# Layer norms of a tower: all eight chunks in one group, with four rows in each of four blocks of 32 partitions

## The chip, the cores and the metric

The kernel runs on one core of a Trainium2 chip. The metric is the time of one execution on the device, in microseconds (us). The engines are named as the profile names them: PE is TensorE (matmuls), PEld its weight load, DVE is VectorE, ACT is ScalarE, POOL is GpSimd, SP is SyncE, which issues the DMAs of this kernel.

## What is computed

The reference is a tower of eight residual stages after a convolution with its normalization, on a tensor h of 4 batches, 746 positions and 128 channels. Ahead of each of the eight stages stands a plain layer norm over the 128 channels. Three of the steps hold a further layer norm with a gain and an offset for each channel: one at the end of the first mixture of experts, and one at the start and one at the end of the last. Cut to what the change touches:

```python
def layer_norm(x, g, b):
    m = x.mean(-1, keepdims=True)
    v = ((x - m) ** 2).mean(-1, keepdims=True)
    return (x - m) / jnp.sqrt(v + EPS) * g + b

h = _L0_tok_ref(x, ...)
h = h + _L0_attn_ref(_layernorm(h, axis=-1), ...)
h = h + _L0_ffn_ref(_layernorm(h, axis=-1), ...)
...
h = h + _L3_ffn_ref(_layernorm(h, axis=-1), ...)
```

## The kernel before

The activations lie with the channels on the 128 partitions: `hT` is 128 x 2984 (4 batches of 746), `zT` holds the normalized copy. A layer norm is a block of its own: `Alloc.clear` ends each block with a barrier over all engines (line 74), so nothing of the stage before or behind it runs beside it. There are eleven such blocks: eight plain ones (names `ln1` to `ln8` in the code, shown together as `ln_...` by the profile), `ln_ffn` and `ln_out` with gain, offset and an addition to `hT` (`add=True`), and `ln_in` with gain and offset, written to `zT`.

Within a block the 2984 columns are eight chunks of 373 (`HALF`), each of them half a batch. For a chunk, PE multiplies by the matrix `center`, which gives the deviations from the mean in a bank `d` of PSUM (line 233); ACT squares them to `sq` (line 274) and copies them to `dev` in SBUF (line 278); PE sums the squares over the channels with a weight of five columns, `avg_rows`, of which one is 1/128, so that chunk c of a group lands in row c of the tile `var` (line 240). When all chunks of a group are in, ACT takes the root of the whole tile (line 283) and DVE the reciprocal (line 302). PE then spreads row c over 128 partitions with a weight of 3 or 5 rows, `spread_rows` (line 252), into one of three banks `r_ps`, and DVE multiplies `dev` by it (line 308). With a gain and an offset DVE applies them next (line 312) and, with `add`, adds the result to `hT` (line 315).

The eight chunks are in two groups, `LN_GROUPS = ((0, 3), (3, 8))`. The order on each engine is written out by hand: the deviations of three chunks, the variances of group 0, further deviations, then the variances of group 1. The second group's chain runs beside the first one's. Everything is float32, and a float32 matmul stands in the profile as two records of MATMUL and two of LDWEIGHTS.

`load_constants` (line 99) is the first block of the program: SP loads five constants, DVE clears `zT`, and the next block's loads start behind its barrier.

## Time and profile before

| | |
|---|---|
| time, median of 3 runs | 3778.83 us (3778.07 to 3781.88) |
| time of the profiled execution | 3788.9 us |
| its span | 3786.8 us |
| PE busy | 3283.6 us, 87% of the span |
| DVE busy | 2044.3 us, 54% |
| ACT busy | 1478.5 us, 39% |
| mean granted TensorE clock | 0.894 of 2.4 GHz |

The span is the stretch in which the engines work; the time of the same execution is 2.1 us more. Busy shares are means over stages with different limits. PE's busy time counts a matmul from its start to its modelled end, so matmuls in a pipeline overlap, and their starts tell more of their pace than their durations do. A granted clock of 1.00 is 2.4 GHz, 0.50 is 1.2 GHz.

### The profile page before, as it was taken

How to read it: one execution, taken by the hardware profiler on the slowest of the kernel's cores; microseconds unless marked ns; L12 is line 12 of the kernel's file. 1: busy time of each engine (PE TensorE's matmuls, PEld its weight loads, DVE VectorE, ACT ScalarE, POOL GpSimd, SP SyncE). 2: the span in 40 equal slices, each digit the busy share in tenths (PEclk: the TensorE clock that was granted, in tenths of full speed). 3: DMA queues.
4: the chain of work that ended last, by engine and by line, in shares of the span. 5: the costliest groups of instructions: out<-in, count | busy, mean ns of one | idle time of the engine just before them, and what ended most of it. 6: DMA issues, size and time to landing. Idle time of an engine off the chain costs nothing. (4 is left out here: it accounts for less than half of the span.)

```text
span 3786.8 us, 48812 instructions
## 1 busy us (share of the span) xinstructions
PE 3283.6 (87%) x15986; PEld 2080.6 (55%) x15986; DVE 2044.3 (54%) x4128; ACT 1478.5 (39%) x2951; POOL 25.2 (1%) x56
## 2 busy tenths in 40 slices
PE   6399999995799989977598869999859999977997
PEld 3244444443577768834254446666536666645775
DVE  3355665662499981054314347776646777743223
ACT  2145555542244431122241215555415555533443
POOL 0000000000000000000000000000000000000000
PEclk8599999996799999978696669999969999977998
DMA  2344444430111110000010031222023333201110
GB/s 83 113 132 136 137 133 140 134 122 22 48 45 67 44 35 18 0 2 0 11 34 0 0 128 61 75 107 112 10 79 81 70 71 75 51 2 69 45 67 19
DMA packets 138473, 243.98 MB, mean 64 GB/s; under 512 B 44389, under 2 KB 106215, under 8 KB 132548
## 3 DMA queue, kind: packets, MB, share of 16 engines
q1 hardware_dynamic: 130982, 232.85, 19.3%
q10 hardware_dynamic: 7360, 9.44, 0.8%
q8 instruction: 75, 1.23, 0.1%
q14 instruction: 56, 0.46, 0.0%
HBM read 147.39 MB, written 57.67 MB: 54 GB/s over the span
## 5 line engine op out<-in xcount | busy, mean ns | idle before, releaser
L1176 PE MATMUL moe_o_ps<-moe_hid,moe_w 128*128 128x373 f32 x1152 | 387.6, 479 | 14.2 <-DVE moe_hid L1244 14.2
L398 PE MATMUL moe_h_ps<-stage_z_part,moe_wh 128*128 128x374 f32 x1152 | 340.0, 376 | 5.2 <-ACT stage_y L1191 1.7
L2111 ACT ACTIVATE lstm_gate<-lstm_g_ps,lstm_bias 128x373 f32<-128x373 f32 x368 | 209.8, 573 | 250.2 <-PE lstm_g_ps L2072 236.5
L894 DVE TENSOR_REDUCE rel_nmax<-rel_s_ps 128x1 f32<-128x746 f32 x192 | 179.1, 933 | 197.6 <-PE rel_s_ps L751 153.1
L1176 PEld LDWEIGHTS moe_o_ps<-moe_hid,moe_w 128*128 128x128 f32 x1152 | 216.1, 190 | 126.6 <-issue 18.5
L2710 DVE TENSOR_REDUCE caus_nmx<-caus_a_ps 128x4 f32<-128x512 f32 (+5 forms) x352 | 215.8, 641 | 107.5 <-PE caus_a_ps L2526 104.8
L858 ACT ACTIVATE rel_probs<-rel_s_ps,rel_nmax 128x746 f32<-128x746 f32 x192 | 169.7, 884 | 258.0 <-DVE rel_nmax L894 153.2
L2072 PE MATMUL lstm_g_ps<-lstm_state,lstm_w 128*128 128x373 f32 x640 | 254.6, 480 | 6.7 <-DVE lstm_state L2194 4.1
L1202 ACT ACTIVATE moe_ex<-moe_h_ps,moe_w 128x373 f32<-128x373 f32 x320 | 173.1, 574 | 221.2 <-PE moe_h_ps L398 219.7
L2661 ACT ACTIVATE caus_probsT<-caus_s_ps 128x512 f32<-128x512 f32 (+4 forms) x352 | 189.6, 558 | 150.8 <-PE caus_s_ps L2545 147.1
L398 PEld LDWEIGHTS moe_h_ps<-stage_z_part,moe_wh 128*128 128x128 f32 x1152 | 209.8, 192 | 55.3 <-DVE moe_hid L1244 12.8
L2066 PE MATMUL lstm_g_ps<-lstm_xm,lstm_w 128*128 128x373 f32 x512 | 202.3, 477 | 0.0
L1229 DVE TENSOR_TENSOR moe_part<-moe_o_ps,moe_gate 128x373 f32<-128x373 f32 x144 | 78.1, 542 | 229.0 <-PE moe_o_ps L1176 229.0
L1244 DVE SCALAR_TENSOR_TENSOR moe_hid<-moe_h_ps,moe_w,moe_ex 128x373 f32<-128x373 f32 x320 | 194.0, 606 | 11.3
L398 PE MATMUL moe_h_ps<-stage_z_part,moe_wl 128*128 128x374 f32 x576 | 194.8, 338 | 0.0
L1204 ACT ACTIVATE moe_hid<-moe_h_ps,moe_w 128x373 f32<-128x373 f32 x256 | 135.4, 573 | 144.6 <-PE moe_h_ps L398 144.6
L2526 PE MATMUL caus_a_ps<-caus_ks,caus_qs 96*128 96x128 f32 (+6 forms) x768 | 180.2, 326 | 10.5 <-DVE caus_nmx L2710 10.5
L2545 PE MATMUL caus_s_ps<-caus_qs,caus_ks 98*128 98x128 f32 (+6 forms) x768 | 186.3, 333 | 0.5 <-ACT caus_probsT L2661 0.4
L762 PE MATMUL rel_t_ps<-tower_ident,rel_probs 128*128 128x128 f32 x1152 | 167.4, 284 | 4.5 <-DVE rel_probsT L657 4.5
L2072 PEld LDWEIGHTS lstm_g_ps<-lstm_state,lstm_w 128*128 128x128 f32 x640 | 122.1, 191 | 87.1 <-DVE lstm_state L2194 4.7
L398 PE MATMUL shared_h_ps<-stage_z_part,shared_w1h 128*128 x576 | 147.6, 338 | 13.2 <-DVE shared_w1l L390 13.0
L789 PE MATMUL rel_o_ps<-rel_probsT,rel_v_pad 128*32 128x373 f32 x768 | 150.8, 501 | 0.2 <-issue 0.2
(385 smaller groups left out, 5677.0 us busy)
## 6 DMA issues: line engine op xcount, KB each, us to landing
moe_gate<-gates SPq DMA_DIRECT2D x18, 1536.0 KB, 7.0
lstm_row<-gates SPq DMA_DIRECT2D x16, 1536.0 KB, 13.4
caus_qs<-caus_xh SPq DMA_DIRECT2D x128, 93.2 KB, 2.1
caus_ks<-caus_xh SPq DMA_DIRECT2D x128, 93.2 KB, 2.1
moe_w<-in_moe_w SPq DMA_DIRECT2D x18, 514.0 KB, 3.6
lstm_row<-gates SPq DMA_DIRECT2D x8, 1152.0 KB, 7.4
rel_shear<-rel_probs SPq DMA_DIRECT2D x32, 256.0 KB, 3.0
rel_bias<-rel_r_sb SPq DMA_DIRECT2D x32, 255.0 KB, 2.0
```

Source lines behind the costliest of these rows:

```text
L398: mm = nc.tensor.matmul(out, w[i], x[j], start=(start and n == 0), stop=(stop and n == len(terms) - 1))
L894: nc.vector.tensor_reduce(nmax[now.slot][:, t:t + 1], s_ps[t % 2][:, 0:L], AX.X, ALU.max, negate=True).then_inc(max_ready, 1)
L1176: mm = nc.tensor.matmul(o_ps[i % 2][:, 0:HALF], w[s][:, HID + j * P:HID + (j + 1) * P], hid[i % 2][:, j, :], start=(j == 0), stop=(j == HJ ...
L1202: nc.scalar.activation(ex[j][:], h_ps[j][:, 0:HALF], ACT.Exp, bias=b1).then_inc(ex_done, 1)
L1244: nc.vector.scalar_tensor_tensor(out=hid[i % 2][:, j, :], in0=h_ps[j][:, 0:HALF], scalar=w[s][:, 2 * HID + j:2 * HID + j + 1], in1=ex[j][: ...
L2066: mm = nc.tensor.matmul(bank, w[e % 2][:, g * P:(g + 1) * P], z, start=True, stop=(s == 0))
L2072: mm = nc.tensor.matmul(bank, w[e % 2][:, 4 * P + g * P:4 * P + (g + 1) * P], state[e % 2][k or 0][i][:], start=False, stop=True)
L2111: nc.scalar.activation(gate[x % 3][g][:], g_ps[n % RING][:, 0:HALF], ACT.Tanh if g == 2 else ACT.Sigmoid, bias=b[:, e, g:g + 1]).then_inc( ...
L2526: mm = nc.tensor.matmul(out[:, at, :], qs[s][0:K_S, hh, t * P:q1], ks[s][0:K_S, hh, k0:k1], start=not diag, stop=not diag or hh == HPG - 1)
L2545: mm = nc.tensor.matmul(out[:, at, :], ks[s][0:K_T, hh, j * P:k1], qs[s][0:K_T, hh, q0:q1], start=not diag, stop=not diag or hh == HPG - 1)
L2661: nc.scalar.activation(probsT[j][0:rows, heads[0]:heads[-1] + 1, q0 - j * P:q1 - j * P], heads_of(s_ps[at % 3][0:rows, :], heads, q1 - q0) ...
L2710: nc.vector.tensor_reduce(nmx[0:rows, slot, heads[0]:heads[-1] + 1, t:t + 1], heads_of(bank[0:rows, :], heads, k1 - k0), AX.X, ALU.max, ne ...
```

## The change

A block has one group of all eight chunks. A chunk's 373 columns are cut into two halves of 187 (`SUB`), the second starting at column 186 (`SUB_AT`). The tile `var` is now 128 partitions by 187 columns: chunk c = 4g + j has its two halves in rows 32j + 2g and 32j + 2g + 1, so each block of 32 partitions holds four rows that are used. The weight of the variance, `avg_sel`, has 32 columns, and its four matmuls of a row (j = 0 to 3) write to the four blocks of 32 partitions. There is one root and one reciprocal, of 128 x 187. To spread a chunk, PE takes 32 rows of `spread_sel` and of `rstd`, in two matmuls of 187 columns, into one of four banks `r_ps`; the banks `d` are three instead of four. The copies from `d` to `dev` are moved from ACT to DVE, and each waits for its chunk's square. With a gain, `spread_sel` is replaced by a tile of the block that holds the gain in place of the ones (128 x 512, loaded in the block), and the offset is added by DVE together with `hT` in one instruction (line 307 of the changed kernel), or by ACT for `ln_in` (line 286). `load_constants` clears the two selection tiles on DVE first, SP waits for that, and then fills them with five small loads in place of two.

```diff
-LN_GROUPS = ((0, 3), (3, 8))
+SUB_AT = HALF // 2
+SUB = HALF - SUB_AT
...
-            for name in ("center", "avg_rows", "spread_rows"):
-                sp.dma_start(K[name][:], io[name]).then_inc(loaded, 16)
-            sp.wait_ge(loaded, 80)
+            sp.dma_start(K["center"][:], io["center"]).then_inc(loaded, 16)
+            sp.wait_ge(cleared, 2)
+            sp.dma_start(K["avg_sel"][:, :, 0:4], io["avg_rows"][:, 0:4, 0:4]).then_inc(loaded, 16)
+            for j in range(4):
+                sp.dma_start(K["spread_sel"][32 * j:32 * j + 4, :, :], io["spread_rows"][0:4, 0:4, :]).then_inc(loaded, 16)
+            sp.wait_ge(loaded, 128)
...
+            nc.vector.memset(K["avg_sel"][:], 0.0).then_inc(cleared, 1)
+            nc.vector.memset(K["spread_sel"][:], 0.0).then_inc(cleared, 1)
             nc.vector.memset(K["zT"][:], 0.0).then_inc(filled, 1)
...
-def layer_norm(nc, K, name, src="hT", affine=None, affine_d=None, add=False):
+def layer_norm(nc, K, name, src="hT", affine_d=None, add=False):
...
-    D, R = 4, 3
+    D, G = 3, 4
+    N = len(CHUNKS)
+    rows_of = 2 * (N // G)
...
-        sd = [a.sb(f"sd{g}", [GROUP_MAX, HALF]) for g in range(2)]
-        rstd = [a.sb(f"rstd{g}", [GROUP_MAX, HALF]) for g in range(2)]
+        sd = a.sb("sd", [P, SUB])
+        rstd = a.sb("rstd", [P, SUB])
+        spread_sel = K["spread_sel"] if affine_d is None else a.sb("spread_scale", [P, rows_of, P])
+        beta = None if affine_d is None else a.sb("beta", [P, 1])
         d = [a.ps(f"d{i}", [P, BANK]) for i in range(D)]
-        var = a.ps("var", [GROUP_MAX, BANK])
-        r_ps = [a.ps(f"r_ps{i}", [P, BANK]) for i in range(R)]
+        var = a.ps("var", [P, BANK])
+        r_ps = [a.ps(f"r_ps{i}", [P, BANK]) for i in range(G)]
...
-            if affine is not None:
-                sp.dma_start(affine[:], affine_d).then_inc(cols_in, 16)
+            if affine_d is not None:
+                sp.dma_start(beta[:], affine_d[1]).then_inc(beta_in, 16)
+                sp.dma_start(spread_sel[:], affine_d[0]).then_inc(scale_in, 16)
...
-            def variance(g, c):
-                first, end = LN_GROUPS[g]
-                pe.wait_ge(sq_ready, c + 1)
-                if g > 0 and c == first:
-                    pe.wait_ge(sd_ready, g)
-                mm = nc.tensor.matmul(var[:, 0:HALF], K["avg_rows"][:, c - first, :], sq[c][:], start=(c == first),
-                                      stop=(c == end - 1))
-                if c == end - 1:
+            def variance(g):
+                pe.wait_ge(sq_ready, (g + 1) * G)
+                for m in range(2):
+                    row = 2 * g + m
+                    for j in range(G):
+                        mm = nc.tensor.matmul(var[32 * j:32 * j + 32, 0:SUB], K["avg_sel"][:, row, :],
+                                              sq[g * G + j][:, m * SUB_AT:m * SUB_AT + SUB], start=(row == 0),
+                                              stop=(row == rows_of - 1))
+                if g == N // G - 1:
                     mm.then_inc(var_ready, 1)
-            def spread_row(g, c):
-                first, end = LN_GROUPS[g]
-                if c == first:
-                    pe.wait_ge(rstd_ready, g + 1)
-                if c >= R:
-                    pe.wait_ge(scaled, c - R + 1)
-                n = end - first
-                nc.tensor.matmul(r_ps[c % R][:, 0:HALF], K["spread_rows"][0:n, c - first, :], rstd[g][0:n, :],
-                                 start=True, stop=True).then_inc(spread, 1)
-            for c in range(LN_GROUPS[0][1]):
+            def spread_row(c):
+                g, j = divmod(c, G)
+                if g > 0:
+                    pe.wait_ge(scaled, c - G + 1)
+                for m in range(2):
+                    nc.tensor.matmul(r_ps[j][:, m * SUB_AT:m * SUB_AT + SUB], spread_sel[32 * j:32 * j + 32, 2 * g + m, :],
+                                     rstd[32 * j:32 * j + 32, :], start=True, stop=True).then_inc(spread, 1)
+            for c in range(0, 5):
                 deviations(c)
-            for c in range(LN_GROUPS[0][1]):
-                variance(0, c)
-            for c in range(D - 1, N - 1):
+            variance(0)
+            for c in range(5, N):
                 deviations(c)
-            variance(1, D - 1)
-            deviations(N - 1)
-            for c in range(D, N):
-                variance(1, c)
-            for g in range(2):
-                for c in range(*LN_GROUPS[g]):
-                    spread_row(g, c)
+            variance(1)
+            if affine_d is not None:
+                pe.wait_ge(scale_in, 16)
+            pe.wait_ge(rstd_ready, 1)
+            for c in range(N):
+                spread_row(c)
...
-            def squares(c0, c1):
-                for c in range(c0, c1):
-                    act.wait_ge(d_ready, c + 1)
-                    nc.scalar.activation(sq[c][:], d[c % D][:, 0:HALF], ACT.Square).then_inc(sq_ready, 1)
-            def copies(c0, c1):
-                for c in range(c0, c1):
-                    nc.scalar.copy(dev[c][:], d[c % D][:, 0:HALF]).then_inc(copied, 1)
-            def roots(g):
-                act.wait_ge(var_ready, g + 1)
-                n = LN_GROUPS[g][1] - LN_GROUPS[g][0]
-                nc.scalar.activation(sd[g][0:n, :], var[0:n, 0:HALF], ACT.Sqrt, bias=K["eps5"][0:n, 0:1]).then_inc(sd_ready, 1)
-            squares(0, LN_GROUPS[0][1])
-            copies(0, LN_GROUPS[0][1])
-            roots(0)
-            squares(LN_GROUPS[0][1], D)
-            copies(LN_GROUPS[0][1], D)
-            squares(D, N)
-            roots(1)
-            copies(D, N)
+            def squares(c):
+                act.wait_ge(d_ready, c + 1)
+                nc.scalar.activation(sq[c][:], d[c % D][:, 0:HALF], ACT.Square).then_inc(sq_ready, 1)
+            for c in range(N):
+                squares(c)
+            act.wait_ge(var_ready, 1)
+            nc.scalar.activation(sd[:], var[:, 0:SUB], ACT.Sqrt, bias=K["eps5"][:, 0:1]).then_inc(sd_ready, 1)
+            if affine_d is not None and not add:
+                act.wait_ge(beta_in, 16)
+                for c, (b, half) in enumerate(CHUNKS):
+                    act.wait_ge(scaled, c + 1)
+                    nc.scalar.activation(z_chunk(zT, b, half), xn[c % 2][:], ACT.Identity, bias=beta[:, 0:1]).then_inc(moved, 1)
...
-            if affine is not None:
-                dve.wait_ge(cols_in, 16)
-            link = Chain(dve, chain)
-            for g, (first, end) in enumerate(LN_GROUPS):
-                n = end - first
-                dve.wait_ge(sd_ready, g + 1)
-                nc.vector.reciprocal(rstd[g][0:n, :], sd[g][0:n, :]).then_inc(rstd_ready, 1)
-            for c, (b, half) in enumerate(CHUNKS):
-                dve.wait_ge(spread, c + 1)
-                x = xn[c % 2][:]
-                out = z_chunk(zT, b, half) if affine is None else x
+            def copies(c):
+                dve.wait_ge(sq_ready, c + 1)
+                nc.vector.tensor_copy(dev[c][:], d[c % D][:, 0:HALF]).then_inc(copied, 1)
+            def multiply(c):
+                b, half = CHUNKS[c]
+                out = z_chunk(zT, b, half) if affine_d is None else xn[c % 2][:]
                 dve.wait_ge(copied, c + 1)
-                nc.vector.tensor_tensor(out, dev[c][:], r_ps[c % R][:, 0:HALF], ALU.mult).then_inc(scaled, 1)
-                if affine is not None:
-                    dve.wait_ge(scaled, c + 1)
-                    out = x if add else z_chunk(zT, b, half)
-                    link.link(nc.vector.tensor_scalar(out, x, affine[:, 0:1], affine[:, 1:2], ALU.mult, ALU.add))
-                    if add:
-                        h = h_chunk(hT, b, half)
-                        link.link(nc.vector.tensor_tensor(h, h, x, ALU.add))
+                dve.wait_ge(spread, 2 * (c + 1))
+                if affine_d is not None and c > 1:
+                    dve.wait_ge(moved, c - 1)
+                nc.vector.tensor_tensor(out, dev[c][:], r_ps[c % G][:, 0:HALF], ALU.mult).then_inc(scaled, 1)
+            def add_to_h(c):
+                b, half = CHUNKS[c]
+                h = h_chunk(hT, b, half)
+                dve.wait_ge(scaled, c + 1)
+                nc.vector.scalar_tensor_tensor(h, xn[c % 2][:], beta[:, 0:1], h, ALU.add, ALU.add).then_inc(moved, 1)
+            def finish_chunk(c):
+                multiply(c)
+                if add and c > 0:
+                    add_to_h(c - 1)
+            for c in range(N):
+                copies(c)
+            if add:
+                dve.wait_ge(beta_in, 16)
+            dve.wait_ge(sd_ready, 1)
+            nc.vector.reciprocal(rstd[:], sd[:]).then_inc(rstd_ready, 1)
+            for c in range(N):
+                finish_chunk(c)
+            if add:
+                add_to_h(N - 1)
...
-            "avg_rows": a.sb("avg_rows", [P, GROUP_MAX, GROUP_MAX]),
-            "spread_rows": a.sb("spread_rows", [GROUP_MAX, GROUP_MAX, P]),
+            "avg_sel": a.sb("avg_sel", [P, 4, 32]),
+            "spread_sel": a.sb("spread_sel", [P, 4, P]),
...
+def spread_scale(g):
+    out = np.zeros((P, 4, P), np.float32)
+    for m in range(4):
+        out[m::32, m, :] = g
+    return out
```

Left out are the hunks that only pass the gain and the offset from the host in two arrays.

On PE, the first plain layer norm, between the token convolution and the attention. Before:

```order
L233 MATMUL ln_d<-tower_hT,tower_center 128x373 x3
L240 MATMUL ln_var<-ln_sq,tower_avg_rows 5x373 x3
L233 MATMUL ln_d<-tower_hT,tower_center 128x373 x4
L240 MATMUL ln_var<-ln_sq,tower_avg_rows 5x373
L233 MATMUL ln_d<-tower_hT,tower_center 128x373
L240 MATMUL ln_var<-ln_sq,tower_avg_rows 5x373 x4
L252 MATMUL ln_r_ps<-ln_rstd,tower_spread_rows 128x373 x8
```

With the change:

```order
L239 MATMUL ln_d<-tower_hT,tower_center 128x373 x5
L246 MATMUL ln_var<-ln_sq,tower_avg_sel 32x187 x8
L239 MATMUL ln_d<-tower_hT,tower_center 128x373 x3
L246 MATMUL ln_var<-ln_sq,tower_avg_sel 32x187 x8
L257 MATMUL ln_r_ps<-ln_rstd,tower_spread_sel 128x187 x16
```

Five deviations come ahead of the first variances, the eight variance matmuls of 373 columns are sixteen of 187, in two runs of eight, and the eight spreads are sixteen of half the width.

On DVE, the last layer norm, at the end of the program. Before (rows 3 to 5 then come for each chunk):

```order
L302 RECIPROCAL ln_out_rstd<-ln_out_sd 3x373
L302 RECIPROCAL ln_out_rstd<-ln_out_sd 5x373
L308 TENSOR_TENSOR ln_out_xn<-ln_out_dev,ln_out_r_ps 128x373
L312 TENSOR_SCALAR ln_out_xn<-ln_out_xn,stage_ln_cols 128x373
L315 TENSOR_TENSOR tower_hT<-tower_hT,ln_out_xn 128x373
```

With the change (the last two rows then alternate to the end):

```order
L292 COPY ln_out_dev<-ln_out_d 128x373 x8
L319 RECIPROCAL ln_out_rstd<-ln_out_sd 128x187
L301 TENSOR_TENSOR ln_out_xn<-ln_out_dev,ln_out_r_ps 128x373 x2
L307 SCALAR_TENSOR_TENSOR tower_hT<-ln_out_xn,ln_out_beta,tower_hT 128x373
L301 TENSOR_TENSOR ln_out_xn<-ln_out_dev,ln_out_r_ps 128x373
```

The eight copies come to DVE, one reciprocal goes, and a chunk has two instructions behind the reciprocal instead of three; the addition of a chunk stands behind the multiply of the next.

## Rows read from the trace of the kernel before

**Rows 1.** The page: the span, and each engine's busy time.

```profile
span 3786.8 us, 48812 instructions
...
PE 3283.6 (87%) x15986; PEld 2080.6 (55%) x15986; DVE 2044.3 (54%) x4128; ACT 1478.5 (39%) x2951; POOL 25.2 (1%) x56
```

**Rows 2.** Line 308, eight plain norms: what it waited for (us, times).

```profile
  PE ln_r_ps L252: 19.5, 30
```

**Rows 3.** Timeline, first norm A: start, duration (us), engine, work, idle before, releaser.

```profile
46.99 4.07 PE L233 MATMUL ln_d<-tower_hT,tower_center 128*128 128x373 f32 x6 [5.89 <-PEq L74]
...
57.43 2.67 PE L240 MATMUL ln_var<-ln_sq,tower_avg_rows 128*5 128x373 f32 x8
...
60.14 0.56 ACT L283 ACTIVATE ln_sd<-ln_var,tower_eps 5x373 f32<-5x373 f32 x1 [2.12 <-PE ln_var L240]
...
63.14 2.70 DVE L308 TENSOR_TENSOR tower_zT<-ln_dev,ln_r_ps 128x373 f32<-128x373 f32 x5
...
69.02 0.54 DVE L308 TENSOR_TENSOR tower_zT<-ln_dev,ln_r_ps 128x373 f32<-128x373 f32 x1 [0.70 <-PE ln_r_ps L252]
```

**Rows 4.** Timeline, the plain norm B at 1796.5 us.

```profile
1796.57 2.12 PE L233 MATMUL ln_d<-tower_hT,tower_center 128*128 128x373 f32 x6 [1.52 <-PEq L74]
1797.47 1.74 ACT L274 ACTIVATE ln_sq<-ln_d 128x373 f32<-128x373 f32 x3 [11.79 <-PE ln_d L233]
...
1808.16 2.48 DVE L302 RECIPROCAL ln_rstd<-ln_sd 5x373 f32<-5x373 f32 x1 [3.45 <-ACT ln_sd L283]
```

**Rows 5.** Timeline, `ln_out`: table load and root, a chunk on DVE, the end.

```profile
3756.76 1.28 ACT L283 ACT_TABLE_LOAD   x1
...
3764.58 2.48 DVE L302 RECIPROCAL ln_out_rstd<-ln_out_sd 5x373 f32<-5x373 f32 x1 [3.37 <-ACT ln_out_sd L283]
...
3766.99 0.47 DVE L308 TENSOR_TENSOR ln_out_xn<-ln_out_dev,ln_out_r_ps 128x373 f32<-128x373 f32 x1
...
3768.59 0.55 DVE L308 TENSOR_TENSOR ln_out_xn<-ln_out_dev,ln_out_r_ps 128x373 f32<-128x373 f32 x1
...
3779.72 0.55 DVE L315 TENSOR_TENSOR tower_hT<-tower_hT,ln_out_xn 128x373 f32<-128x373 f32 x1
```

**Rows 6.** Timeline, `ln_in`: its second reciprocal and its last instruction.

```profile
3389.50 2.48 DVE L302 RECIPROCAL ln_in_rstd<-ln_in_sd 5x373 f32<-5x373 f32 x1 [4.30 <-ACT ln_in_sd L283]
...
3400.05 0.48 DVE L312 TENSOR_SCALAR tower_zT<-ln_in_xn,stage_ln_cols 128x373 f32<-128x373 f32 x1
```

**Rows 7.** Stretches of norms A and B: us, busy times, then PEclk (granted clock), DMA.

```profile
46.96:51.40 4.44, 4.41 (x7) 1.94 (x8) 0.00 (x0) 1.27 (x3) 0.00 (x0) 0.50 0.00 0
51.60:65.10 13.50, 11.91 (x37) 4.61 (x36) 6.70 (x6) 6.32 (x15) 0.00 (x0) 1.00 0.00 0
65.20:69.57 4.37, 3.79 (x7) 1.51 (x5) 2.18 (x4) 0.00 (x0) 0.00 (x0) 0.50 0.00 0
1796.54:1812.70 16.16, 14.54 (x43) 6.01 (x44) 6.80 (x6) 8.68 (x19) 0.00 (x0) 1.00 0.00 1
```

**Rows 8.** Lines of other stages with like work: ns minimum/median/maximum, starts, shapes.

```profile
L2742 DVE RECIPROCAL caus_r<-caus_su x128: 679/727/741, 2871.7 to 3344.3; 128x93 f32<-128x93 f32 x96, 128x94 f32<-128x94 f32 x32
...
L906 DVE COPY rel_o_sb<-rel_o_ps x16: 539/540/541, 238.4 to 861.6; 64x373 f32<-64x373 f32 x16
...
L1890 DVE SCALAR_TENSOR_TENSOR tower_hT<-picked_eo,stage_weight_cols,tower_hT x16: 606/607/610, 1887.4 to 1964.9; 128x373 f32<-128x373 f32 x16
...
L2651 ACT COPY caus_su<-caus_a_ps x32: 354/471/586, 2865.2 to 3339.7; 128x512 f32<-128x512 f32 x16, 128x234 f32<-128x234 f32 x16
```

**Rows 9.** Timeline, PE in the causal attention, at clock 1.00.

```profile
2923.42 1.40 PE L2561 MATMUL caus_o_ps<-caus_probsT,caus_v_tok 128*32 128x128 f32 x32
```

**Rows 10.** Timeline, the program's start.

```profile
1.47 2.62 DVE L117 MEMSET tower_zT<- 128x3080 f32 x1 [1.47 <-PEq L2831]
...
2.61 0.38 SPq L112 DMA_DIRECT2D tower_spread_rows<-in_spread_rows  x1
...
4.99 0.36 SPq L143 DMA_DIRECT2D tok_w<-in_tok_w  x1
```

More of the change, by code:

```diff
@@ L103, in load_constants @@
         loaded = a.sem("loaded")
+        cleared = a.sem("cleared")
         filled = a.sem("filled")
@@ L1427, in stage2 @@
         shared_conv(nc, io, K, y, z_parts)
-        layer_norm(nc, K, "ln_ffn0", src=y, affine=cols, affine_d=io["ln_ffn0"], add=True)
+        layer_norm(nc, K, "ln_ffn0", src=y, affine_d=(io["ln_ffn0_g"], io["ln_ffn0_b"]), add=True)
 STAGES[2] = stage2
@@ L1536, in _ @@
                 dve.wait_ge(done, B)
-        layer_norm(nc, K, "ln_out3", src=y, affine=cols, affine_d=io["ln_out3"], add=True)
+        layer_norm(nc, K, "ln_out3", src=y, affine_d=(io["ln_out3_g"], io["ln_out3_b"]), add=True)
 STAGES[8] = stage8
@@ L1547, in stage8_layout @@
         "moe3_b2": f["L3_ffn_b2"],
-        "ln_in3": np.stack([f["L3_ffn_ln_g"], f["L3_ffn_ln_b"]], 1),
-        "ln_out3": np.stack([f["L3_ffn_out_g"], f["L3_ffn_out_b"]], 1),
+        "ln_in3_g": spread_scale(f["L3_ffn_ln_g"]),
+        "ln_in3_b": f["L3_ffn_ln_b"][:, None],
+        "ln_out3_g": spread_scale(f["L3_ffn_out_g"]),
+        "ln_out3_b": f["L3_ffn_out_b"][:, None],
     }
```

14 lines of the change are left out of this document (6 added, 8 removed).

## The prediction

> **What bounds the kernel now.** I read the page first. PE is busy for 3283.6 of 3786.8 us and DVE for 2044.3 [rows 1], but the change touches only the eleven layer norms, which stand between barriers, so shares over the whole span say nothing here. The question is how long each norm's own chain is: what it saves there is saved in full, since nothing runs beside it.
>
> So the timelines of the norms come next. Norm A, the first, starts at 46.99 and ends at 69.02 + 0.54 = 69.56: 22.6 us. Its chain has three parts [rows 3]. The front runs from the first matmul to the second root, which starts at 60.14, 13.15 us in. On it PE is nearly always at work: the last eight records of the variance start at 57.43, and the root follows 2.71 us later. Then root and second reciprocal: 0.56 and 2.48 us. Then the tail, 69.56 − (60.14 + 0.59 + 2.48) = 6.35 us, in which five multiplies take 2.70 us without a pause and the last waits 0.70 us for PE.
>
> Norm B starts with PE at 2.4 GHz, and its first square starts 0.90 us after the first matmul; its second reciprocal starts 11.6 us in [rows 4], where A's starts 13.7 us in. The stretches say why: A's first 4.4 us have a granted clock of 0.50, B's first 16 us have 1.00. In A the clock is back at 0.50 for the last 4.4 us [rows 7], and there the multiplies wait for PE: the eight plain norms wait 19.5 us in all, 30 times [rows 2].
>
> In `ln_out` the tail is 3780.27 − 3767.06 = 13.2 us, because DVE has three instructions for a chunk, one chunk each (3768.59 − 3766.99) = 1.60 us at the start [rows 5]. In `ln_in`, with two instructions, it is 3400.53 − 3391.98 = 8.55 us [rows 6].
>
> **The front.** A float32 matmul of 373 columns is two records. The eight variance records of A take 2.67 us and B's first six 2.12 [rows 3, 4]: both fit 0.31 us for a record and some 0.2 us of modelled end behind the last, so 0.62 us for a matmul. At a clock of 0.50 it is twice that, 1.24 us: A's first six records take 4.07 us.
>
> The variance goes from 8 x 0.62 = 5.0 us to sixteen matmuls of 187 columns, which in a row would take the same 5.0 us. But they lie in four blocks of 32 columns of the array. The causal attention has such work: 32 records of 128 x 128, with 32 columns of weight, in 1.40 us [rows 9]; in a row they would take 32 x 128 / 373 x 0.31 = 3.4 us and more. So four blocks do run at the same time there. By that row a run of eight matmuls (16 records of 187 columns) takes 16/32 x 1.22 (without the last end) x 187/128 = 0.9 us at most; four at a time exactly would be 0.63 us. I take 0.65 us, for the order of the loops is the same, j inside. That is 1.3 us instead of 5.0 for both runs, but PE now waits for squares, which it did not before.
>
> I walk through B with the new order. Deviations 0 to 2 end at 1.9 us. The fourth needs bank 0 free: square 0 ends at 0.9 + 0.5 = 1.4, and the copy, now on DVE and behind the square, costs 0.54 us by a like copy from PSUM [rows 8], so 2.0; it ends at 2.7, the fifth at 3.35. Square 3 ends at 3.5, the first variances run from 3.6 to 4.3, deviations 5 to 7 from 4.4 to 6.3, square 7 from 6.6 to 7.1, the second variances from 7.2 to 7.85. The root can start at 8.1. Before it stood at 11.0 (0.59 us ahead of the reciprocal, as in A): 2.9 us less. In A, where the clock rises near 4.5 us, the fifth deviation ends at 5.4, deviation 7 at 8.3, square 7 at 9.1, and the root starts at 10.1 instead of 13.15: 3.0 us less. One thing is late next: in seven norms ACT loads a table of 1.28 us for the root [rows 5]. Before, it lay beside the first group's work; now it starts at the end of square 7, and the root at 7.1 + 1.3 = 8.4. So I take −3.0 for four norms and −2.7 for seven: **−30.9 us**. If the copies on DVE cost twice as much they would still end ahead of PE's other work in A, and cost 0.5 us in B.
>
> **Root and reciprocal.** On ACT, 512 columns take 586 ns and 234 take 354 [rows 8], 0.83 ns a column, so 186 fewer columns are 0.15 us less: **−1.7 us** over eleven. The reciprocal is 2.48 us for 373 columns whether 3 or 5 partitions, and 0.72 for 93 with 128 partitions [rows 4, 8]; on the line between, 187 columns cost 1.31 us. One instead of two, and the first was beside other work: −1.17 each, **−12.8 us**.
>
> **The tail.** All eight spreads now stand behind the reciprocal, where three of them were ahead of it. The first multiply waits for 0.62 us of matmul and its way through, 1.0 us in all, by B's first square [rows 4]. That is a cost that was not there. Behind it the multiplies follow one another if PE keeps up: 2.70 / 5 = 0.54 us each [rows 3], 4.3 us for eight. PE needs 0.63 us for a chunk at full clock if its matmuls run one after another, and less if chunks overlap. The chunks lie in four blocks of rows, and no row of this trace shows blocks of rows beside one another; only blocks of columns are shown. Bounds: 0.16 us a chunk with four at a time, 0.63 at 2.4 GHz in a row, 1.25 at 1.2 GHz in a row. I take overlap, since rows 9 are the nearest. Then the plain tail is 5.35 us. Before it was 6.35 in A; over eight norms the multiplies waited 19.5 / 8 = 2.4 us each [rows 2], and 4.3 + 2.4 less the overlap at the first is 6.6 us. **−1.25 x 8 = −10.0 us**.
>
> The Trainium skill, page "TensorE: Matmul & The Clock Gate", section "Part 3: Packing small matmuls — row/col tiling", says the same of rows: four tiles of 32 rows ran 3.07 times as fast as one after another. By the Trainium skill's figure a chunk would cost 0.63 / 3.07 = 0.2 us, an estimate; one after another it is 0.63. No row here shows blocks of rows, and the sum is made without that figure.
>
> With `add` a chunk is 0.57 us of multiply and 0.61 + 0.02 of the fused addition [rows 8], 1.2 x 8 + 1.0 = 10.7 us against 13.2: **−5.0 us** for two. In `ln_in` the offset moves to ACT beside the next multiply: 1.0 + 8 x 0.57 + 0.65 = 6.3 against 8.55: **−2.2 us**. The gains' load is issued as the block starts and needed eight microseconds later, so it costs nothing; without that cover it would be some 3 us three times.
>
> **The constants.** Before, the last of five loads is issued at 2.61 and the next block's first at 4.99; the clearing of `zT` ends at 4.09 [rows 10], so both paths were level. Now 640 columns are cleared first, by 2.62 us for 3080 columns some 0.6 us; SP goes on at 2.15, issues five loads 0.47 us apart, the last at 4.1 instead of 2.61: **+1.5 us**.
>
> **The sum**: −30.9 − 1.7 − 12.8 − 10.0 − 5.0 − 2.2 + 1.5 = −61.1 us. The profiled execution (3788.9 us, its span and 2.1 us around it) would become 3727.8. The median of the runs shown is 10.1 us lower, and the same difference gives 3778.8 − 61.1 = **3718 us**. Chance of this case 0.70. By its own bounds it lies between 3706 (a chunk in B-like norms always at full clock, the front 0.5 us shorter each) and 3736.
>
> **Rivals.** *The spreads run one after another, and the clock falls in the tail* (0.13). For it: no row shows blocks of rows at the same time, and PE idles for some 2.1 us before the spreads, the root and the reciprocal. Against: in A the clock held from 4.6 to 18.1 us [rows 7], longer than the new norm lasts. With every spread at 1.25 us the plain tail is 1.7 + 7 x 1.25 + 0.55 = 11.0 us, +4.4 against before, so eight plain norms give back 45 us, and the others 5: 3768 us. With half of the tails so, 3743.
>
> *The column blocks do not overlap* (0.05): each of the two runs takes 2.5 us instead of 0.65, +3.7 us a norm, 3759 us. Rows 9 speak against it. This is the case in which the change does not do what it says, since the packed layout would buy only the shorter reciprocal.
>
> *No change that can be told* (0.04): the first rival in full and a fifth of the second, 3776 us.
>
> *Slower* (0.04): one mechanism, PE stays at 1.2 GHz in the whole norm because it now works in short bursts, and spreads in a row. Eight deviations take 9.9 us, the root starts at 14.0 instead of 13.15 (or 11.0, in a norm like B), the plain tail is 11.0: about +1.3 at the front, −1.3, +4.4, so +4.4 a plain norm, +4 over the three others, +1.5: 3819 us. It decides from about 1.3 us for a spread chunk on: below that the front's 3 us and the reciprocal pay for the tail. B's sixteen microseconds at 1.00 with pauses in them speak against it.
>
> *More than forecast* (0.04), below 3706: the clock is high in more norms, since they are shorter.
>
> **The numbers.** Range 3704 to 3746, which holds the forecast's own bounds and half of the first rival. A difference under 0.2%, 7.6 us, is about what a measurement of this kernel can't tell from none: 3771.3 to 3786.4. Faster 0.92, same 0.04, slower 0.04.
>
> **What would show it.** In the profile after: roots in norms like A near 10.1 to 10.4 us after the first matmul; a reciprocal near 1.3 us; variance records in runs of eight matmuls of 0.65 us and its pipeline end; multiplies 0.54 to 0.57 us apart with no wait for PE but the first; token weights asked for near 6.5 us instead of 4.99. The forecast is wrong if multiplies wait for the spreads, if the copies on DVE hold up the deviations, or if the granted clock is 0.50 over whole norms.

## The result and the profile after

The changed kernel takes 3728.45 us (median of four runs, 3726.81 to 3733.92), the kernel before 3780.36 us beside it: a ratio of 0.9863, with a 95% interval of 0.9846 to 0.9880, so 51.9 us less. The forecast was 3718 us, with a range of 3704 to 3746.

The page of the changed kernel, to be read beside [rows 1]:

```profile
span 3732.1 us, 49417 instructions
...
PE 3216.6 (86%) x16290; PEld 2084.7 (56%) x16338; DVE 2039.7 (55%) x4183; ACT 1446.7 (39%) x2860; POOL 25.2 (1%) x56
```

The profiled execution took 3733.92 us, 55.0 less than that of before, and its span is 54.7 us shorter. DVE's busy time hardly moves: in each norm eight copies come to it, while two long reciprocals become one short one. The eleven norms, each from its first matmul to its last instruction, add up to 199.1 us instead of 258.4. So the norms give 59.3 us, and 4.6 us are given back outside them.

The timeline of the norm that answers to B [rows 4]. At the end of a row stands the idle time of the engine before it, and what ended it:

```profile
1779.80 3.54 PE L239 MATMUL ln_d<-tower_hT,tower_center 128*128 128x373 f32 x10 [1.48 <-PEq L75]
...
1783.29 0.84 PE L246 MATMUL ln_var<-ln_sq,tower_avg_sel 128*32 128x187 f32 x16
1784.06 2.15 PE L239 MATMUL ln_d<-tower_hT,tower_center 128*128 128x373 f32 x6
...
1786.75 1.28 ACT L281 ACT_TABLE_LOAD   x1
...
1786.79 0.84 PE L246 MATMUL ln_var<-ln_sq,tower_avg_sel 128*32 128x187 f32 x16 [0.57 <-ACT ln_sq L276]
1788.05 0.42 ACT L281 ACTIVATE ln_sd<-ln_var,tower_eps 128x187 f32<-128x187 f32 x1
1788.49 1.33 DVE L319 RECIPROCAL ln_rstd<-ln_sd 128x187 f32<-128x187 f32 x1 [1.18 <-ACT ln_sd L281]
...
1789.88 1.65 PE L257 MATMUL ln_r_ps<-ln_rstd,tower_spread_sel 32*128 32x187 f32 x16 [2.25 <-DVE ln_rstd L319]
1791.60 1.90 DVE L301 TENSOR_TENSOR tower_zT<-ln_dev,ln_r_ps 128x373 f32<-128x373 f32 x4 [1.78 <-PE ln_r_ps L257]
...
1793.92 1.90 DVE L301 TENSOR_TENSOR tower_zT<-ln_dev,ln_r_ps 128x373 f32<-128x373 f32 x4 [0.42 <-PE ln_r_ps L257]
```

The root starts 1788.05 − 1779.80 = 8.25 us after the first matmul (forecast 8.4) and the reciprocal takes 1.33 us (1.31). Sixteen variance records take 0.84 us with their end. Then the surprise: the first multiply waits 1.78 us behind the reciprocal, not 1.0, and the fifth waits 0.42. The first four multiplies start (1.90 − 0.54) / 3 = 0.45 us apart.

Stretches of 1 us at the first spreads, in six of the eleven norms (columns as in [rows 7]):

```profile
62.00:63.00 1.00, 1.00 (x12) 1.00 (x16) 0.00 (x0) 0.00 (x0) 0.00 (x0) 0.50 0.08 16
909.50:910.50 1.00, 0.86 (x16) 0.57 (x16) 0.07 (x1) 0.00 (x0) 0.00 (x0) 1.00 0.00 0
...
1789.90:1790.90 1.00, 1.00 (x12) 1.00 (x16) 0.00 (x0) 0.00 (x0) 0.00 (x0) 0.50 0.00 0
1953.30:1954.30 1.00, 1.00 (x12) 1.00 (x16) 0.00 (x0) 0.00 (x0) 0.00 (x0) 0.50 0.00 0
...
2719.10:2720.10 1.00, 0.86 (x16) 0.57 (x16) 0.07 (x1) 0.00 (x0) 0.00 (x0) 1.00 0.00 0
...
3715.50:3716.50 1.00, 0.94 (x16) 0.66 (x16) 0.02 (x1) 0.00 (x0) 0.00 (x0) 1.00 0.00 0
```

The number right behind the five busy times, the granted clock, is 0.50 in three of these rows. Of all eleven norms, seven are so, and four have 1.00. Where it is 1.00, the first multiply waits 1.06 to 1.13 us and a plain tail takes 5.28 us; where it is 0.50, 1.78 to 1.84 and 6.00. What line 301 (the multiply) waited for over the plain norms (us, times), beside 19.5 and 30 in [rows 2]:

```profile
  PE ln_r_ps L257: 15.8, 17
```

In `ln_out` the clock was 1.00 at the spreads, and DVE alone sets the pace, 1.20 us a chunk instead of 1.60 [rows 5]:

```profile
3718.12 0.54 DVE L301 TENSOR_TENSOR ln_out_xn<-ln_out_dev,ln_out_r_ps 128x373 f32<-128x373 f32 x1
3718.59 0.60 DVE L307 SCALAR_TENSOR_TENSOR tower_hT<-ln_out_xn,ln_out_beta,tower_hT 128x373 f32<-128x373 f32 x1
3719.32 0.55 DVE L301 TENSOR_TENSOR ln_out_xn<-ln_out_dev,ln_out_r_ps 128x373 f32<-128x373 f32 x1
```

The start of the program, beside [rows 10]; the load of `tok_w` is issued 1.1 us later than before:

```profile
2.62 1.43 SPq L117 DMA_DIRECT2D tower_spread_sel<-in_spread_rows  x4
...
6.10 0.36 SPq L150 DMA_DIRECT2D tok_w<-in_tok_w  x1
```

The terms in us, summed over the eleven norms of the two profiled executions (the measured sum is that of the unrounded terms). The front runs from the first matmul to the root, the tail from the end of the reciprocal to the last instruction:

| term | forecast | measured |
|---|---|---|
| front, to the (second) root | −30.9 | −32.1 |
| root | −1.7 | −1.5 |
| reciprocal | −12.8 | −12.7 |
| tail, eight plain norms | −10.0 | −6.3 |
| tail, `ln_ffn` and `ln_out` | −5.0 | −5.1 |
| tail, `ln_in` | −2.2 | −1.7 |
| outside the norms | +1.5 | +4.6 |
| sum | −61.1 | −54.7 |

### The profile page after: what moved, and what is told of

The parts are those of the page before. It is cut to its first block and busy times, and to the rows that moved or that the text cites. A ratio compares the mean times of both kernels' runs of the same rounds, so it can differ in the third digit from the quotient of the medians.

```text
span 3732.1 us, 49417 instructions
## 1 busy us (share of the span) xinstructions
PE 3216.6 (86%) x16290; PEld 2084.7 (56%) x16338; DVE 2039.7 (55%) x4183; ACT 1446.7 (39%) x2860; POOL 25.2 (1%) x56
## 5 line engine op out<-in xcount | busy, mean ns | idle before, releaser
L406 PEld LDWEIGHTS moe_h_ps<-stage_z_part,moe_wh 128*128 128x128 f32 x1152 | 210.0, 192 | 54.9 <-DVE moe_hid L1252 12.8
L406 PE MATMUL shared_h_ps<-stage_z_part,shared_w1h 128*128 x576 | 148.2, 339 | 12.4 <-DMA shared_b<-in_sh_b 12.4
```

Source lines behind the costliest of these rows:

```text
L406: mm = nc.tensor.matmul(out, w[i], x[j], start=(start and n == 0), stop=(stop and n == len(terms) - 1))
```

## The experiments

The theory after the first comparison is that both kinds of blocks overlap, and that the plain tail was mis-sized because PE idles before the spreads and then runs them at 1.2 GHz. A rival for the late first multiply is a cost of the row blocks themselves. Each edit is made to the changed kernel. A ratio is to the kernel before on the same chip, whose median there was 3786.3 us (`col_serial`, `row_serial`, `fill_pe`, `whole_consts`), 3792.0 (`change_again`, `best`, `copies_act`, `one_group_rows`) or 3790.5 (`fill_one`, `offset_apart`) and not 3780.4, so ratios are compared, and medians only within such a set; sums over the norms are against the changed kernel's first profile.

**col_serial**: the variance's weight is 128 columns wide, so its matmuls can't lie beside one another.

```diff
-    mm = nc.tensor.matmul(var[32 * j:32 * j + 32, 0:SUB], K["avg_sel"][:, row, :],
...
+    at = P - 1 - (32 * j + row)
+    mm = nc.tensor.matmul(var[:, 0:SUB], K["avg_strip"][:, at:at + P],
...
```

> The changed kernel with one thing undone: the variance matmuls take a weight of 128 columns (cut from a strip, the 1/128 in column 32j + row), so all of them use the same block of columns of PE and cannot run beside one another. Count and widths stay (16 matmuls of 187 columns a norm). Theory (the blocks of 32 columns do run four at a time, and the variance lies on the front's chain): each run of eight takes 2.5 us instead of the 0.84 of the changed kernel's profile, the root comes 3.3 us later in each of eleven norms, some 36 us more in all, less up to 5 us if the clock stays high longer: +31 to +36 us, about 3760 to 3765. Rival (squares and copies set the front, PE's variance hides beside them): under 10 us more.

Measured: 3758.07 us (3757.33 to 3765.36), ratio 0.9928 [0.9911, 0.9945]. In the norm like B a run of eight variance matmuls became:

```profile
1794.18 2.80 PE L252 MATMUL ln_var<-ln_sq,tower_avg_strip 128*128 128x187 f32 x16
```

It is 2.80 us instead of 0.84, twice a norm, and the fronts grow by 2.2 to 3.7 us each, 35.6 in all. The norms together grow by 31.1, since the clock was high at more of the spreads. A record now takes some 0.16 us, the same pace as the 0.31 us for 373 columns with a weight of five columns [rows 3], so it is the lost overlap that costs and not the wider weight. The packing of columns carries about half of what the norms gain.

**row_serial**: spread weights of 128 rows, zero outside the one that is wanted.

```diff
-    nc.tensor.matmul(r_ps[j][:, m * SUB_AT:m * SUB_AT + SUB], spread_sel[32 * j:32 * j + 32, 2 * g + m, :],
-                     rstd[32 * j:32 * j + 32, :], start=True, stop=True).then_inc(spread, 1)
+    nc.tensor.matmul(r_ps[j][:, m * SUB_AT:m * SUB_AT + SUB], spread_sel[:, 4 * j + 2 * g + m, :],
+                     rstd[:, :], start=True, stop=True).then_inc(spread, 1)
```

> The changed kernel with one thing undone: the spreads take a weight of 128 rows (a single one, or gain, in it) and all 128 rows of rstd, so chunks can't run beside one another. Count and widths stay (16 matmuls of 187 columns). The weights are larger (1 MB once and for each norm with a gain). Theory (the four blocks of rows run beside one another): chunks come 1.25 us apart at 1.2 GHz and 0.63 at 2.4. The tail of a plain norm goes from 6.0 to 10.9 us where the clock is low and from 5.3 to 6.0 where it is high: about +30 us over eleven norms, 3758. Rival (PE takes one block after the other in the changed kernel as well): within 3 us of it.

Measured: 3743.72 us (3739.56 to 3750.27), ratio 0.9891 [0.9874, 0.9907]. The tails grow by 12.4 us, and the norms by 11.1. (The larger weights also let the first norm start 2.1 us later, so the tails are compared and not the medians.) DVE's timeline in the norm like B, and PE's row from the next norm, whose tail has a clock of 1.00:

```profile
1796.43 0.55 DVE L299 TENSOR_TENSOR tower_zT<-ln_dev,ln_r_ps 128x373 f32<-128x373 f32 x1 [1.78 <-PE ln_r_ps L255]
1797.67 0.54 DVE L299 TENSOR_TENSOR tower_zT<-ln_dev,ln_r_ps 128x373 f32<-128x373 f32 x1 [0.70 <-PE ln_r_ps L255]
1798.43 3.71 DVE L299 TENSOR_TENSOR tower_zT<-ln_dev,ln_r_ps 128x373 f32<-128x373 f32 x6 [0.22 <-PE ln_r_ps L255]
...
1959.42 5.33 PE L255 MATMUL ln_r_ps<-ln_rstd,tower_spread_sel 128*128 128x187 f32 x32 [2.25 <-DVE ln_rstd L317]
```

The first multiply waits the same 1.78 us for one chunk in a row as it did for four side by side. At a clock of 1.00 it waits 1.07 us here and 1.06 in the changed kernel. So the rival falls: the row blocks cost nothing, and the clock sets the wait. The next multiply starts 1.24 us behind the first, the price of a spread at 1.2 GHz; from 1797.7 on the granted clock is 1.00 again and the rest wait little. The expected size was too large because it left that return out, which came within five chunks in every low norm. In the last row 32 records one after another take 5.33 us. The first 16 of them take 2.80 with their end, against 0.94 at the same clock for 16 in four row blocks (a row of `fill_pe`, below): 3.0 times. The Trainium skill, page "TensorE: Matmul & The Clock Gate", section "Part 3: Packing small matmuls — row/col tiling", gives 3.07 for four tiles of 32 rows; by that, the trace agrees in kind and nearly in size, though the page's figure is for wider matmuls.

**fill_pe**: three idle matmuls, that is matmuls whose result nobody reads, between the variances and the spreads, into a free bank.

```diff
+FILL = 3
...
+            pe.wait_ge(copied, N - 1)
+            for _ in range(FILL):
+                nc.tensor.matmul(d[0][:, 0:HALF], K["center"][:], x_chunk(0), start=True, stop=True)
             pe.wait_ge(rstd_ready, 1)
```

> The changed kernel plus three matmuls of 373 columns behind the variance, into a bank of d that is free by then, whose result nobody reads: PE works while ACT takes the root and DVE the reciprocal. Theory (the tail came out longer than forecast because the granted clock is 0.50 when the spreads come, in eight of eleven norms, since PE idles before them): the clock stays at 1.00, the first multiply starts 1.06 us behind the reciprocal instead of 1.78, and the stall of 0.5 us before the fifth goes: −0.7 us in eight norms, −5.7 us, about 3723. Rival (the banks r_ps and DVE set the tail): clock up, tail unchanged. Second rival (the added matmuls delay the spreads): +0.3 us a norm.

Measured: 3714.42 us (3709.56 to 3718.30), ratio 0.9804 [0.9791, 0.9818]. The norm like B, timeline (the first row holds the three idle matmuls, six records), and two stretches at its spreads, the second over its whole tail:

```profile
1781.90 2.15 PE L271 MATMUL ln_d<-tower_hT,tower_center 128*128 128x373 f32 x6
...
1784.22 0.94 PE L258 MATMUL ln_r_ps<-ln_rstd,tower_spread_sel 32*128 32x187 f32 x16 [0.17 <-DVE ln_rstd L323]
1785.23 3.34 DVE L305 TENSOR_TENSOR tower_zT<-ln_dev,ln_r_ps 128x373 f32<-128x373 f32 x7 [1.06 <-PE ln_r_ps L258]
```

```profile
1784.30:1785.30 1.00, 0.86 (x16) 0.57 (x16) 0.07 (x1) 0.00 (x0) 0.00 (x0) 1.00 0.00 0
```

```profile
1784.20:1789.40 5.20, 3.91 (x32) 3.13 (x32) 3.84 (x8) 0.00 (x0) 0.00 (x0) 0.79 0.00 0
```

PE's idle time before the spreads falls from 2.25 to 0.17 us, the clock is 1.00 at the first spreads in all eleven norms, and the first multiply waits 1.06 to 1.18. Seven multiplies run without a pause between them. (The expectation speaks of eight low norms in the changed kernel; the rows show seven.) The tails shrink by 7.8 us. So the clock is shown to be the cause of the long first wait and of the stall at the fifth chunk.

The idle matmuls do not keep the clock up for good, they make it fall later. By the last row its mean is 0.79 over the whole tail: here it fell 3.0 us after the first spread, and the eighth multiply waited 0.34 us for that. Over the eleven norms it fell 3.0 to 6.3 us after the first spread, while the last spread of a plain norm is through after 3.9 to 4.6.

On the same chip `whole_consts`, which differs from the change in its first block alone, takes 12.1 us more, and the tails explain only part of that. The fronts shrink by 2.7, most of it in two norms whose clock also rose at other times in other executions, and the profile has 5.1 us less outside the norms, where nothing was changed. The edit can't claim either part.

**fill_one**: the same with one idle matmul (the edit is shown against `fill_pe`).

```diff
-FILL = 3
+FILL = 1
```

> As fill_pe, with one added matmul instead of three, so that PE works for 0.6 us of the 2.1 us between variance and spreads. Theory (what counts is that PE works through the gap): most of the eight plain norms with spreads at 0.50 keep it, tails as in the changed kernel (5.3 to 6.0 us), median under 3 us below it. Rival (any matmul in the gap is enough): tails near 4.9 us and the time of fill_pe, some 10 us below.

Measured: 3725.24 us (3720.35 to 3733.37), ratio 0.9827 [0.9802, 0.9852]. Three of eleven norms were low at the first spreads, and the tails 3.1 us shorter than with the change. One matmul does not do the work of three. Whether it does anything is not settled, since the change itself, run again (next), had five low norms.

**change_again**: the changed kernel as it is, profiled and timed once more, with no edit.

> The changed kernel itself, once more, on the same chip as the next three. Expected from its first timing: 0.986 of the kernel before. In its profile each norm whose spreads start at a granted clock of 0.50 should have its first multiply 1.78 us behind the reciprocal, each at 1.00 1.06 us; what lies between the norms should add up to 3520 to 3527 us, as in the profiles so far.

Measured: 3727.74 us (3720.07 to 3729.80), ratio 0.9828 [0.9811, 0.9844]. The stretches at the spreads of four norms:

```profile
1605.80:1606.80 1.00, 0.94 (x16) 0.65 (x16) 0.02 (x1) 0.00 (x0) 0.00 (x0) 1.00 0.00 0
1628.50:1629.50 1.00, 0.93 (x16) 0.64 (x16) 0.00 (x1) 0.00 (x0) 0.00 (x0) 1.00 0.00 0
1788.70:1789.70 1.00, 1.00 (x12) 1.00 (x16) 0.00 (x0) 0.00 (x0) 0.00 (x0) 0.50 0.00 0
...
2720.00:2721.00 1.00, 1.00 (x12) 1.00 (x16) 0.00 (x0) 0.00 (x0) 0.00 (x0) 0.51 0.00 0
```

Five norms are low here, and not the same ones: the first two of these were low before, the last was high. But "high" holds for the first spreads only. The tail of the second of these norms, in two longer stretches:

```profile
1628.20:1630.50 2.30, 1.34 (x18) 1.06 (x19) 1.24 (x4) 0.00 (x0) 0.00 (x0) 1.00 0.00 0
1630.50:1634.00 3.50, 2.56 (x16) 2.07 (x14) 2.90 (x6) 0.00 (x0) 0.00 (x0) 0.60 0.00 0
```

The clock falls here too, 2.7 us after the first spread, and two of the later multiplies come late by it. It falls in all 22 norms of the two profiles of this kernel: in the twelve low ones between 0.8 us before the first spread and 0.1 us after it, in the ten others 1.5 to 2.7 us after it. The norms' sum is only 1.0 us less, but outside them this profile has 3.3 us less than the first, 3530.0 and 3533.4 us. (Without the 6.5 us behind the last norm it is 3523.6, within the expectation's bounds.) So the number of low norms belongs to the execution, and a difference of 3 us outside the norms says nothing. Over all eleven profiles of kernels with one group, whose code outside the norms differs in the first block at most, it runs from 3524.0 to 3533.5 us. The two ratios of the same kernel, 0.9863 and 0.9828, differ by more than their intervals suggest: its own median moved by 0.7 us, that of the kernel before by 11.7.

**whole_consts**: the two selection tiles come whole from the host in two loads, nothing is cleared for them.

```diff
-            sp.wait_ge(cleared, 2)
-            sp.dma_start(K["avg_sel"][:, :, 0:4], io["avg_rows"][:, 0:4, 0:4]).then_inc(loaded, 16)
-            for j in range(4):
-                sp.dma_start(K["spread_sel"][32 * j:32 * j + 4, :, :], io["spread_rows"][0:4, 0:4, :]).then_inc(loaded, 16)
+            sp.dma_start(K["avg_sel"][:], io["avg_sel"]).then_inc(loaded, 16)
+            sp.dma_start(K["spread_sel"][:], io["spread_sel"]).then_inc(loaded, 16)
```

> The changed kernel with avg_sel and spread_sel loaded whole, zeros included, in two loads, so that nothing is cleared and SP does not wait. Theory (the clearing, the wait and the three further loads cost at the program's start): the token weights are asked for at 5.0 us instead of 6.10, the token input lands 1.1 to 1.9 us earlier, and the first norm starts some 2 us earlier: −1 to −3 us. Rival (the larger load takes as long): no change at the start.

Measured: 3726.49 us (3719.51 to 3730.64), ratio 0.9836 [0.9821, 0.9850], not to be told from the change. Its start, and what the last constant takes to land (last number):

```profile
2.61 0.43 SPq L114 DMA_DIRECT2D tower_spread_sel<-in_spread_sel  x1
...
5.97 0.33 SPq L145 DMA_DIRECT2D tok_w<-in_tok_w  x1
```

```profile
tower_spread_sel<-in_spread_sel SPq DMA_DIRECT2D x1, 256.0 KB, 2.6
```

The last load is issued as early as before, but it now has 256 KB, and the next block's load starts only 0.13 us earlier than with five small ones (6.10), still 1.0 us later than before (4.99).

**best**: `fill_pe`, `whole_consts`, and one early root of a 128 x 1 tile behind the fifth square, so that the table is loaded there.

```diff
-            for c in range(N):
+            for c in range(5):
+                squares(c)
+            nc.scalar.activation(early[:], K["eps5"][:, 0:1], ACT.Sqrt)
+            for c in range(5, N):
                 squares(c)
```

> The changed kernel with three additions: the three idle-time matmuls of fill_pe, the constants of whole_consts, and a root of one column on ACT between the fifth and the sixth square, so that the table load (1.28 us) lies in ACT's pause there and not ahead of the root. Theory (the three costs are apart and add up): fill_pe was 0.6% below the changed kernel's ratio, the constants save 1 to 2 us, and the table 0.25 us in seven norms, 1.7 us: a ratio near 0.979 to the kernel before. Rival (the early load pushes the last squares back by as much as it saves): root no earlier in the seven norms, ratio as fill_pe with the constants, 0.980.

Measured: 3716.19 us (3708.49 to 3717.51), ratio 0.9793 [0.9777, 0.9810]. On the same chip `change_again` had no run below 3720.07, so this version beats both kernels; from `fill_pe` it can't be told apart. ACT in the norm like B:

```profile
1778.10 1.28 ACT L280 ACT_TABLE_LOAD   x1
1779.40 0.20 ACT L280 ACTIVATE ln_early<-tower_eps 128x1 f32<-128x1 f32 x1
...
1781.92 0.42 ACT L284 ACTIVATE ln_sd<-ln_var,tower_eps 128x187 f32<-128x187 f32 x1 [0.96 <-PE ln_var L243]
```

The root starts 7.9 us into the norm instead of 8.25, which is the 0.3 us that the forecast gave for the table. But the reciprocal now ends before the three idle matmuls are quite through, and the first multiply waits 1.17 us instead of 1.06. Two would perhaps do; that wasn't tried.

**copies_act**: the copies back on ACT, each behind its square.

```diff
                 nc.scalar.activation(sq[c][:], d[c % D][:, 0:HALF], ACT.Square).then_inc(sq_ready, 1)
+                nc.scalar.copy(dev[c][:], d[c % D][:, 0:HALF]).then_inc(copied, 1)
...
-            for c in range(N):
-                copies(c)
```

> The changed kernel with one thing undone: the copies from d to dev are on ACT again, each behind its square. Theory (the copies had to leave ACT for the short front, since a square and a copy are 0.94 us a chunk against PE's 0.62): the last square comes 0.6 us later where a norm starts at 1.2 GHz and 1.2 us later where it starts at 2.4, and the root waits for the last copy too: +0.7 to +1.6 us a norm, +8 to +17 us. Rival (the wait for squares hides it, either engine does): within 3 us of the changed kernel.

Measured: 3733.44 us (3729.59 to 3734.54), ratio 0.9844 [0.9826, 0.9862]. ACT in the norm like B, the first chunks:

```profile
1783.62 0.48 ACT L276 ACTIVATE ln_sq<-ln_d 128x373 f32<-128x373 f32 x1 [11.61 <-PE ln_d L239]
1784.00 0.47 ACT L277 COPY ln_dev<-ln_d 128x373 f32<-128x373 f32 x1
1784.35 0.50 ACT L276 ACTIVATE ln_sq<-ln_d 128x373 f32<-128x373 f32 x1
```

A pair of square and copy starts 0.73 us after the pair before it, not the 0.95 that their durations add up to, so the last square is only 0.39 us later. The last copy then puts the table load off, and the root is 0.8 us later in the norms that start at 2.4 GHz; the fronts lose 5.0 us in all. So the copies on DVE are worth some 5 us in the profile, less than expected; the ratio's interval overlaps that of `change_again`.

**one_group_rows**: one group of eight chunks without the packing. `var` is 8 x 373, the variances and the spreads run in a row, one root and one reciprocal of 8 x 373.

```diff
-                for m in range(2):
-                    row = 2 * g + m
-                    for j in range(G):
-                        mm = nc.tensor.matmul(var[32 * j:32 * j + 32, 0:SUB], K["avg_sel"][:, row, :],
...
+                for c in range(g * G, (g + 1) * G):
+                    mm = nc.tensor.matmul(var[:, 0:HALF], K["avg_sel"][:, c, :], sq[c][:], start=(c == 0), stop=(c == N - 1))
```

> One part of the change alone: all eight chunks in one group with copies on DVE and three banks d, but with one row for a chunk (var is 8 x 373, weights of 8 columns and 8 rows), so neither blocks of columns nor of rows are used and root and reciprocal are over 373 columns. Theory (the packed layout is what pays): the front is 3.2 us longer than the changed kernel's, the root 0.15, the reciprocal 1.15, the tail 1.1 on average: +5.6 us a norm, some +60 us, which makes it as slow as the kernel before or up to 10 us slower (ratio 1.00). Rival (one group with one root is what pays, and the packing only shortens the reciprocal): +1.3 us a norm, ratio 0.990.

Measured: 3817.31 us (3816.59 to 3821.01), ratio 1.0071 [1.0052, 1.0089]: slower than two groups. Its first norm, timeline, and then two stretches:

```profile
63.53 2.48 DVE L308 RECIPROCAL ln_rstd<-ln_sd 8x373 f32<-8x373 f32 x1 [2.78 <-ACT ln_sd L270]
66.06 8.22 PE L247 MATMUL ln_r_ps<-ln_rstd,tower_spread_sel 8*128 8x373 f32 x16 [3.17 <-DVE ln_rstd L308]
```

```profile
64.00:66.00 2.00, 0.00 (x0) 0.00 (x0) 2.00 (x1) 0.00 (x0) 0.00 (x0) 1.00 0.00 0
...
68.00:74.00 6.00, 6.00 (x11) 2.83 (x9) 2.95 (x6) 0.00 (x0) 0.00 (x0) 0.52 0.00 0
```

The norms are 84.2 us longer than with the change: fronts 35.3, reciprocals 12.7, tails 34.6, roots 1.6. The tails cost more than expected, since the clock falls in them: it is still 1.00 while PE idles for 3.17 us, and 0.52 from 2 us after PE has begun again. Against the kernel before, the norms are 24.8 us longer: fronts 3.2, tails 21.5, roots and reciprocals alike. So what one group alone gives up lies nearly all in the tails, where all eight spreads now stand behind the reciprocal; the packing has to pay for that first.

**offset_apart**: multiply, offset and addition are three instructions of DVE again.

```diff
-                nc.vector.scalar_tensor_tensor(h, xn[c % 2][:], beta[:, 0:1], h, ALU.add, ALU.add).then_inc(moved, 1)
+                x = xn[c % 2][:]
+                link.link(nc.vector.tensor_scalar(x, x, beta[:, 0:1], None, ALU.add))
+                nc.vector.tensor_tensor(h, h, x, ALU.add).then_inc(moved, 1)
...
+                if affine_d is not None and not add:
+                    b, half = CHUNKS[c]
+                    dve.wait_ge(scaled, c + 1)
+                    nc.vector.tensor_scalar(z_chunk(zT, b, half), xn[c % 2][:], beta[:, 0:1], None, ALU.add).then_inc(moved, 1)
```

> The changed kernel with one thing undone: the offset is an instruction of its own on DVE in the three norms that have one (in ln_ffn and ln_out ahead of the addition, in ln_in in place of ACT's). Theory (those tails are DVE's): a chunk goes from 1.19 us to 1.19 − 0.61 + 0.48 + 0.55 + 0.03 = 1.64 us, so the tails of ln_ffn and ln_out are 3.6 us longer, that of ln_in 2.5 us, together some 10 us in the profile. Rival (PE's spreads set those tails): no change there.

Measured: 3732.60 us (3730.29 to 3735.27), ratio 0.9845 [0.9824, 0.9865]. In `ln_out` the multiplies are 1.58 us apart instead of 1.20, and its tail is 3.8 us longer, 0.7 of it by a low clock at the first spread; `ln_ffn` loses 3.1 against an execution with the same clock (10.33 in `change_again`), `ln_in` 1.6. That is some 8 us in all, where 10 were expected. With the offset apart the three tails together are 1.1 us longer than in the kernel before, 0.7 of it by the low clock. So the −6.8 us that they gave with the change come from the fused instruction and from ACT's share in `ln_in`, and the forecast's −7.2 was right in kind and nearly in size.

## Why the prediction was right, and which term was off

**The front, root and reciprocal** were right one by one, −45.4 forecast and −46.3 measured. The front was right for the reason given: taking the packing from the columns alone costs 35.6 us of front. The price for the reciprocal, read between two shapes of other lines [rows 4, 8], was 0.02 us off.

**The tail** held the wrong step: "The first multiply waits for 0.62 us of matmul and its way through, 1.0 us in all, by B's first square". That row had the clock at 1.00. In the profile after, seven of eleven norms had 0.50 there, and the wait was 1.78. By the prediction's own signs, "no wait for PE but the first" did not hold: the fifth multiply waited too. The prediction had seen PE idle for 2.1 us before the spreads and the clock at 0.50 in A's old tail [rows 7], but used the fallen clock only in the rival with spreads in a row. That rival's first half was wrong (row blocks overlap) and its second half right. Two smaller errors lay the other way or beside it: the multiplies start 0.45 us apart, not 0.54, and the fifth chunk waits 0.42 us in a low tail for a bank and its spread. At full clock the tail without a stall is 1.06 + 7 x 0.45 + 0.54 = 4.8 us, less than the 5.35 forecast, and `fill_pe` has three tails of 4.78. With the clock at 0.50 from the first spread it is 6.00. Where the clock falls inside the tail it is 5.28, since one or two of the later multiplies come late, by 0.5 us together; that this is near the forecast's 5.35 is luck, two errors that cancel. The eight plain norms give −6.3 instead of −10.0.

**The constants** were +1.5. `tok_w` is asked for 1.1 us later, and the first norm starts 2.7 us later. In `change_again` the load is issued at 6.11, as in the first profile, but the first norm starts at 48.7, only 1.7 later than before. The other microsecond is how the input of the convolution landed in the first execution: its first matmul starts at 16.09 there and at 14.97 in `change_again`. But the agreement of 1.7 with 1.5 is in part luck. The kernels of `copies_act`, `offset_apart`, `fill_one` and `fill_pe` have the same first block, and their first norms start 1.5 to 2.5 us later than before, with convolutions whose matmuls take 27.0 to 28.2 us; before they took 26.9, in one profile. So the cost of the new loads is known to a microsecond only. The remaining 1.9 us outside the norms lie within the 3.3 us by which two profiles of the same kernel differ there.

**The 10 us between forecast and median** are then about 6 from these terms, 3 from the profiled pair (−55.0) against the medians (−51.9), and 1.5 from the kernel before, whose median rose from 3778.8 to 3780.4.

What stays open is what sets the moment at which the clock falls. The last plain norm, with the same pause of 2.25 us, had it 0.4 us before the first spread in one execution and 2.3 us after it in the other. That filling the pause moves the fall behind the first spreads is shown; what decides without the filling is not.

## What to carry to other kernels

Merging groups so that one root and one reciprocal serve all is no gain in itself: it put all spreads behind the reciprocal and lost 0.7%, until the variances and spreads ran in four blocks of the array at once. When a small dependent matmul comes behind a short pause of PE, price it at both clocks, and read the clock at that very place in the trace; three idle matmuls in each pause made this kernel 0.3% faster, 12.1 us, and the tails account for 7.8 us of that. A term taken from a row holds only for that row's clock.

## What the runs showed of the hardware

- Four chunks in four row blocks are ready as soon as one chunk alone: at 1.00, sixteen records of 32 rows and 187 columns take 0.94 us with their end, and the first multiply starts 0.07 us behind that end. One chunk of 128 rows and four chunks of 32 make the first multiply wait equally, 1.07 and 1.06 us at 1.00 and 1.78 us each at 0.50.
- DVE starts a multiply 0.45 us after the last though each is recorded as 0.54 us, and ACT, in `copies_act`, a square or copy 0.35 to 0.38 us after the last, recorded as 0.47 to 0.58.
- The granted clock follows what PE did before with a delay: in the first norm of `one_group_rows` it stays at 1.00 through a pause of 3.17 us and is 0.52 behind it, while PE is busy all the time.
- In the changed kernel it fell in every norm, during a pause of 1.9 to 2.4 us or up to 2.7 us after it. A plain tail took 6.00 us where the fall came at the first spread or before it, 5.28 where it came some 2 us later, and 4.78 where three idle matmuls put it behind the last spread.
